# A fused two-FFN and mixer block on one core: another order and other engines for the loading stage

## The chip, the core and the metric

The kernel runs on one core of one Trainium2 chip. Its engines are TensorE (PE in the profile; PEld are its weight loads), VectorE (DVE), ScalarE (ACT), GpSimd (POOL) and SyncE (SP, which here only issues DMAs). Each works through its own list of instructions in order, and semaphores tie the lists together. PSUM, which TensorE writes, has eight banks of 128 x 512 float32. In this kernel GpSimd's operands all lie in SBUF. The metric is the device time in microseconds (us) of one execution, the median of several.

## What is computed

4096 tokens of 128 features go through three residual steps: a mixture-of-experts FFN, a mixer (gate, a 5-tap convolution, a linear recurrence, an output projection, a layer norm) and the same FFN again. All of it is float32. The FFN, with T tokens, 32 experts of 64 hidden units and a shared expert of 128:

```python
logits = tokens @ router_weight.T
scores = sigmoid(logits);  sfc = scores + router_bias
# the best 2 of 4 groups by the sum of their 2 best scores, then the best 4 experts of these
topk_w = scores[chosen] / (sum of them + 1e-20) * 2.5
hidden = silu(tokens @ gate_w[e].T) * (tokens @ up_w[e].T)        # every expert e
mixed  = sum over the chosen e of topk_w * (hidden @ down_w[e].T)
shared = (silu(tokens @ shared_gate_w.T) * (tokens @ shared_up_w.T)) @ shared_down_w.T
x = x + 0.5 * (mixed + shared)                                    # tokens = layernorm(x)
```

The kernel computes every expert for every token and multiplies by a routing weight that is zero for those not chosen.

## The kernel before

**Tiling.** The tokens are 8 blocks of 512. FFN 1 and FFN 4 (the second) of each block make 16 units (`ORDER`), the first four being FFN 1 of blocks 0 to 3. A unit has 17 tiles (`NT`): tile 0 is the shared expert, tiles 1 to 16 are pairs of experts. For a tile TensorE makes a gate and an up product (`up_tiles`, three matmuls of 512 columns each) and three tiles later a down product (`down`). Between them ScalarE takes the silu in place in the gate's bank (`silu_tile`), VectorE multiplies by the routing weights (`weigh_tile`) and by the up product (`hidden_tile`, into one of four `hid` buffers), and the result is split for the next product.

**The split.** Every operand of a matmul is kept as two numbers of type float32r: a high part (a rounding copy, `xT_hi`, `hid_hi`, `wt_hi`, by ScalarE) and a low part, the difference (`xT_lo`, `wt_lo` by VectorE, `hid_lo` by GpSimd). A product is high x high + high x low + low x high.

**The loading stage.** The weights come from HBM as 14 batches of four 128 x 128 tiles (`raw`); `BATCHES` orders them: number 0 is the mixer's and router's weights, 1 the shared expert's, 2 to 13 the experts'. Each is transposed by TensorE into a PSUM bank (`weights(n)`, L1130), copied to `wt_hi` (`weight_high`, L662) and subtracted to `wt_lo` (`weight_low`, L823, VectorE). Of batches 3 to 5 (`BY_SCALAR`) TensorE itself makes the difference: `weights_rest` (L1120) transposes them again and subtracts the high part by a product with the negated identity, and ScalarE copies it. The low parts 6 to 9 are `LOWS_BEHIND`. Batches 10 to 13 are handled within tiles 1, 3, 5 and 7 of unit 0.

Ahead of them TensorE does 14 transposes of the identity (`WARM`, L1316), whose result nobody reads. Beside the weights, block 0's tokens are normalised by VectorE (L1084), transposed by TensorE (L1325), split, and routed: `first_router` (L1209), 12 products of 32 columns, then `route_step` 0 to 25 on VectorE (L893 to L964, ending in `w_tok`). `transpose_route` (L1224) turns `w_tok`, ScalarE copies it (`wT`, L711), and from there it is spread to all partitions in two ways: the first two pairs (`EARLY`) by products with a spreading matrix (L1348) and two ScalarE copies (L809), the rest by a store to HBM and broadcasting loads (L499, L511) in pieces (`CHUNKS`). `constants` (L1042, VectorE) prepares the mixer's taps, bias and decay, which block 0's mixer needs some 98 us in.

**Order.** All of it is written out by hand; no scheduler moves anything. TensorE's list in the loading stage is: 14 transposes, batch 0, batch 1, the token transposes, batch 2, the router, batches 3 to 9 with `weights_rest` and tile 0's products among them, `transpose_route`, batch 9, the spreading, then the units. Within units tables such as `BEGIN` say beside which tile the norms, routers and the mixer go. Some of the lines:

```python
            weights(0)
            weights(1)
            for t in range(TT):
...
            weights(2)
            first_router()
            for i in range(3, LATE):
```

## Time and profile before

| | us |
|---|---|
| median of 3 runs (lowest, highest) | 674.52 (674.22, 674.72) |
| span of the profiled execution | 672.1 |
| TensorE busy | 658.3 (98%) |
| VectorE busy | 550.3 (82%) |
| GpSimd busy | 447.0 (67%) |
| ScalarE busy | 420.2 (63%) |

The span runs from the first to the last instruction of one profiled execution; the median is of other executions and holds what lies around the span too. A busy share is a mean over stages: 98% on TensorE says that it seldom idles, not that each of its instructions was needed or ran at the full clock. Matmuls overlap, so the distance from one start to the next says more than a duration. Of a wait, the profile names the engine and instruction that came last.

### The profile page before, as it was taken

The page shows a single profiled execution, that of the slowest core. Times are in us where ns is not written, and L with a number is a line of the kernel's source. Part 1 is how long each engine was busy: PE and PEld are TensorE (multiplying, and loading weights), DVE is VectorE, ACT ScalarE, POOL GpSimd, SP SyncE. Part 2 cuts the span into 40 slices and gives each one's busy share as a digit, 9 for nine tenths or more (in the row PEclk, how much of TensorE's full clock was granted, in tenths as well). Part 3 has the DMA queues.
Part 4 walks back from the last instruction along what each step waited for, and adds up shares of the span by engine and source line. Part 5 has one row for each costly group of instructions (what it writes and reads, how often), then busy time and mean ns, then how long its engine had stood idle before and what let it go on. Part 6 is the DMA issues. An engine that isn't in the chain of part 4 may idle for free. (4 is left out here: it accounts for less than half of the span.)

```text
span 672.1 us, 10288 instructions
## 1 busy us (share of the span) xinstructions
PE 658.3 (98%) x3061; PEld 532.4 (79%) x3061; DVE 550.3 (82%) x1542; ACT 420.2 (63%) x802; POOL 447.0 (67%) x452
## 2 busy tenths in 40 slices
PE   7999999999999999999999999999999999999997
PEld 6877888888888887888888888888878778777785
DVE  5788889988978887889779798688989967967765
ACT  3666576675576656666567765767576566655554
POOL 2256557875676776866767766868676776676564
PEclk9999999999999999999999999999999999999999
DMA  8672908439092844619075370916509074380461
GB/s 201 147 159 64 223 1 196 92 76 195 5 213 69 182 89 111 144 57 225 22 173 115 89 166 23 228 38 146 125 25 222 9 156 100 82 188 17 112 143 32
DMA packets 60232, 78.30 MB, mean 117 GB/s; under 512 B 8176, under 2 KB 27664, under 8 KB 60176
## 3 DMA queue, kind: packets, MB, share of 16 engines
q1 hardware_dynamic: 59312, 77.49, 51.8%
q8 instruction: 24, 0.39, 0.3%
q10 hardware_dynamic: 864, 0.15, 0.2%
q14 instruction: 32, 0.26, 0.1%
HBM read 74.49 MB, written 3.15 MB: 116 GB/s over the span
## 5 line engine op out<-in xcount | busy, mean ns | idle before, releaser
L572 POOL TENSOR_TENSOR hid_lo<-hid,hid_hi 128x512 fp32r<-128x512 f32 x270 | 348.8, 1296 | 189.5 <-ACT hid_hi L684 189.3
L837 DVE TENSOR_TENSOR weighted<-gate_ps,raw 128x512 f32<-128x512 f32 x256 | 175.1, 684 | 69.4 <-ACT gate_ps L676 62.5
L676 ACT ACTIVATE gate_ps<-gate_ps 128x512 f32<-128x512 f32 x256 | 148.7, 581 | 120.2 <-PE gate_ps L1118 117.0
L684 ACT ACTIVATE hid_hi<-hid 128x512 fp32r<-128x512 f32 x272 | 170.5, 627 | 62.1 <-DVE hid L850 59.7
L850 DVE TENSOR_TENSOR hid<-weighted,up_ps 128x512 f32<-128x512 f32 x256 | 174.3, 681 | 8.0 <-issue 0.5
L1181 PE MATMUL down_ps<-hid_lo,wt_hi 128*128 128x512 f32 x272 | 107.8, 396 | 0.2 <-DVE hid_lo L858 0.2
L1178 PE MATMUL down_ps<-hid_hi,wt_hi 128*128 128x512 f32 x272 | 107.7, 396 | 0.0
L1179 PE MATMUL down_ps<-hid_hi,wt_lo 128*128 128x512 f32 x272 | 107.5, 395 | 0.0
L1116 PE MATMUL gate_ps<-xT_hi,wt_hi 128*128 128x512 f32 x170 | 71.7, 422 | 0.0
L1116 PE MATMUL up_ps<-xT_hi,wt_hi 128*128 128x512 f32 x170 | 68.2, 401 | 2.1 <-DVE hid L850 2.1
L1117 PE MATMUL gate_ps<-xT_lo,wt_hi 128*128 128x512 f32 x170 | 67.2, 395 | 0.0
L1118 PE MATMUL up_ps<-xT_hi,wt_lo 128*128 128x512 f32 x170 | 67.2, 395 | 0.0
L1117 PE MATMUL up_ps<-xT_lo,wt_hi 128*128 128x512 f32 x170 | 67.1, 395 | 0.0
L1118 PE MATMUL gate_ps<-xT_hi,wt_lo 128*128 128x512 f32 x170 | 67.1, 395 | 0.0
L1181 PEld LDWEIGHTS down_ps<-hid_lo,wt_hi 128*128 128x128 f32 x272 | 51.1, 188 | 13.6 <-DVE hid_lo L858 0.9
L1179 PEld LDWEIGHTS down_ps<-hid_hi,wt_lo 128*128 128x128 f32 x272 | 51.1, 188 | 12.2
L1178 PEld LDWEIGHTS down_ps<-hid_hi,wt_hi 128*128 128x128 f32 x272 | 51.1, 188 | 12.1
L1116 PE MATMUL gate_ps<-xT_hi_spare,wt_hi 128*128 128x512 f32 x102 | 42.5, 417 | 0.0
L1116 PEld LDWEIGHTS up_ps<-xT_hi,wt_hi 128*128 128x128 f32 x170 | 31.9, 188 | 13.2 <-DVE hid L850 5.7
L1116 PE MATMUL up_ps<-xT_hi_spare,wt_hi 128*128 128x512 f32 x102 | 40.4, 396 | 0.0
L1117 PE MATMUL gate_ps<-xT_lo_spare,wt_hi 128*128 128x512 f32 x102 | 40.3, 395 | 0.0
L1118 PE MATMUL up_ps<-xT_hi_spare,wt_lo 128*128 128x512 f32 x102 | 40.3, 395 | 0.0
(187 smaller groups left out, 1111.8 us busy)
## 6 DMA issues: line engine op xcount, KB each, us to landing
raw<-wT_hbm SPq DMA_DIRECT2D x96, 512.0 KB, 11.4
raw<-wT_hbm SPq DMA_DIRECT2D x62, 256.0 KB, 4.5
x_ln<-in_L_attn_x SPq DMA_DIRECT2D x8, 256.0 KB, 3.7
x_res<-in_L_attn_x SPq DMA_DIRECT2D x8, 256.0 KB, 3.3
out_x<-x SPq DMA_DIRECT2D x7, 256.0 KB, 2.3
raw<-in_L_ffn_gate_w SPq DMA_DIRECT2D x4, 256.0 KB, 5.7
raw<-in_L_ffn_up_w SPq DMA_DIRECT2D x4, 256.0 KB, 5.0
raw<-in_L_ffn_down_w SPq DMA_DIRECT2D x4, 256.0 KB, 5.1
```

Source lines behind the costliest of these rows:

```text
L572: nc.gpsimd.tensor_tensor(hid_lo[s][:, :], hid[s][:, :], hid_hi[s][:, :].bitcast(F32), ALU.subtract)\
L676: nc.scalar.activation(bank[:, :] if j else silu_sb[:, :], bank[:, :], ACT.Silu).then_inc(silu_done, 1)
L684: nc.scalar.activation(hid_hi[s][:, :], hid[s][:, :], ACT.Copy).then_inc(hid_hi_done, 1)
L837: V.tensor_tensor(weighted[j % 2][:, :], gate_ps[n % BANKS][:, :], wb[:, j - 1, :], ALU.mult)\
L850: V.tensor_tensor(hid[n % RING][:, :], factor[:, :], up_ps[n % BANKS][:, :], ALU.mult)\
L1116: nc.tensor.matmul(dst, w, moving_hi, start=start, stop=False)
L1117: nc.tensor.matmul(dst, w, moving_lo, start=False, stop=False)
L1118: return nc.tensor.matmul(dst, w_lo, moving_hi, start=False, stop=stop)
L1178: nc.tensor.matmul(down_ps[:, :], wt_hi[:, w, :], hid_hi[s][:, :], start=(j == 0), stop=False)
L1179: nc.tensor.matmul(down_ps[:, :], wt_lo[:, w, :], hid_hi[s][:, :], start=False, stop=False)
L1181: nc.tensor.matmul(down_ps[:, :], wt_hi[:, w, :], hid_lo[s][:, :], start=False, stop=(j == NT - 1)).then_inc(down_done, 1)
```

## The change

It rewrites the loading stage and leaves every product of the 16 units as it is.

- *Warm-up.* The transposes of the identity become products of 512 columns with the negated identity (`warm`): eight ahead of batch 0, two behind it, one behind the token transposes. They wait for `neg_ident` too.
- *Block 0's router ahead of the shared weights.* Batch 1 moves from ahead of the token transposes into `first_router`, between the eight products with the high part and the four with the low part; batch 2 goes behind the router. On ScalarE the tanh of the decay and `xT_high` go ahead of batch 1's copy.
- *Seven low parts on GpSimd.* For batches 1 to 7 (`BY_POOL`) ScalarE copies the transposed batch unrounded into a `hid` buffer (`w_staged`), makes the high part from that, and GpSimd subtracts. `weights_rest` and its copies go. VectorE keeps batches 0 and 8 to 13; its first write into each `hid` buffer waits for all seven (`w_lo_pooled`).
- *Constants on GpSimd*, behind the low parts, with a buffer `half`; block 0's mixer waits for them (`mix_const`).
- *Tile 1 early.* The gate and up products of tile 1 follow tile 0's in the loading stage (batch 8 between them), with both silus ahead of `wT_copy`; `transpose_route` goes behind batch 9. The PSUM banks are assigned anew.

The diff, with declarations and the removed bodies left out:

```diff
-WARM = 14
+WARM = (8, 2, 1)
 
 BATCHES = (0, NBATCH - 1) + tuple(range(1, NBATCH - 1))
 
-BY_SCALAR = range(3, 6)
-
-LOWS_BEHIND = (6, 7, 8, 9)
+BY_POOL = range(1, 8)
+
+LOWS_BEHIND = (8, 9)
...
-        setup_banks = 2 * [gate_ps[0], gate_ps[1], mixed] + [gate_ps[1], up_ps[1], mixed, down_ps] + 4 * [mixed]
-        rest_banks = {3: up_ps[0], 4: up_ps[1], 5: down_ps}
+        setup_banks = [gate_ps[0], gate_ps[1], mixed, up_ps[0], down_ps, gate_ps[1], mixed, down_ps, mixed, down_ps]
+        setup_banks += 4 * [mixed]
...
-                        sp.wait_ge(w_rest, max(min(hi + 1, BY_SCALAR[-1] + 1) - BY_SCALAR[0], 1))
...
+            for i in BY_POOL:
+                pool.wait_ge(w_hi_done, i + 1)
+                nc.gpsimd.tensor_tensor(batch(wt_lo, i), hid[i % RING][:, :], batch(wt_hi, i).bitcast(F32), ALU.subtract)\
+                  .then_inc(w_lo_pooled, 1)
+            mixing = Steps(pool, mix_const, 0)
+            mixing.done(nc.gpsimd.memset(half[:, :], 0.5))
+            pool.wait_ge(taps_loaded, 16 * 3)
+            mixing.wait()
+            mixing.done(nc.gpsimd.tensor_tensor(taps_half[:, :], taps[:, :], half[:, :], ALU.mult))
+            mixing.done(nc.gpsimd.tensor_tensor(cbias_half[:, :], cbias[:, :], half[:, 0:1], ALU.mult))
+            pool.wait_ge(a_done, 1)
+            pool.wait_ge(dve_const, 4)
+            mixing.done(nc.gpsimd.tensor_tensor(decay[:, :], ones[:, :], a_tanh[:, 0:1].broadcast_to([P, BLK]),
+                                                ALU.mult))
+            mixing.wait()
+            mixing.done(nc.gpsimd.memset(decay[:, :].rearrange("p (s t) -> p s t", s=SB)[:, :, 0:1], 0.0))
+            assert mixing.n == MIX_CONST
...
             def weight_high(i):
                 act.wait_ge(w_transposed, i + 1)
-                nc.scalar.activation(batch(wt_hi, i), setup_bank(i), ACT.Copy).then_inc(w_hi_done, 1)
-
-            def weight_low(i):
-                act.wait_ge(w_rest, i - BY_SCALAR[0] + 1)
-                nc.scalar.activation(batch(wt_lo, i), rest_bank(i), ACT.Copy).then_inc(w_lo_copied, 1)
+                whole = setup_bank(i)
+                if i in BY_POOL:
+                    if i - RING in BY_POOL:
+                        act.wait_ge(w_lo_pooled, i - RING - BY_POOL[0] + 1)
+                    whole = hid[i % RING][:, :]
+                    nc.scalar.activation(whole, setup_bank(i), ACT.Copy).then_inc(w_staged, 1)
+                    act.wait_ge(w_staged, i - BY_POOL[0] + 1)
+                nc.scalar.activation(batch(wt_hi, i), whole, ACT.Copy).then_inc(w_hi_done, 1)
...
-                    if before is not None or j > 0:
+                    if before is not None or j > 1:
...
             for i in range(LATE):
                 weight_high(i)
-                if i == 8:
-                    wT_copy(1, 0)
-                    silu_tile(1, 0, 0)
-                if i - 1 in BY_SCALAR:
-                    weight_low(i - 1)
-                if i == 1:
+                if i == 0:
+                    act.wait_ge(taps_loaded, 16 * 3)
+                    nc.scalar.activation(a_tanh[:, :], a_raw[:, :], ACT.Tanh).then_inc(a_done, 1)
                     xT_high(1, 0)
                 if i == 1:
-                    act.wait_ge(taps_loaded, 16 * 3)
-                    nc.scalar.activation(a_tanh[:, :], a_raw[:, :], ACT.Tanh).then_inc(a_done, 1)
-                if i == 2:
                     silu_logits(1, 0)
+                if i == 8:
+                    silu_tile(1, 0, 0)
+                    silu_tile(1, 0, 1)
+                    wT_copy(1, 0)
...
                 if n >= RING:
                     dve.wait_ge(hid_lo_done, n - RING + 1)
+                else:
+                    dve.wait_ge(w_lo_pooled, len(BY_POOL))
...
-            def constants():
...
                     if (k, m) == ORDER[0] and j == 0:
-                        for n in LOWS_BEHIND[2:]:
+                        for n in LOWS_BEHIND:
...
             weight_low(0)
             xT_low(1, 0)
-            weight_low(1)
-            weight_low(2)
-            constants()
...
-            for n in LOWS_BEHIND[:2]:
-                weight_low(n)
...
-            def weights_rest(n):
...
-                if n in (3, 4, 5):
-                    pe.wait_ge(w_lo_done, lows_by_vector(n - 2))
-                elif n == 6:
-                    pe.wait_ge(w_hi_done, 5)
-                elif n == 7:
-                    pe.wait_ge(w_lo_copied, 2)
-                elif n == 8:
-                    pe.wait_ge(w_hi_done, 6)
-                elif n == 9:
-                    pe.wait_ge(w_lo_copied, 3)
+                if n in (5, 6, 7):
+                    pe.wait_ge(w_staged, {5: 1, 6: 2, 7: 4}[n])
+                elif n in (8, 9):
+                    pe.wait_ge(w_staged, n - 2)
                 elif n >= LATE:
                     pe.wait_ge(w_lo_done, lows_by_vector(n))
                 for t in range(4):
-                    last = nc.tensor.transpose(setup_bank(n)[:, t * P:(t + 1) * P],
-                                               raw[:, min(4 * b + t, down_tile(0)), :], ident[:, :])
+                    last = nc.tensor.matmul(setup_bank(n)[:, t * P:(t + 1) * P],
+                                            raw[:, min(4 * b + t, down_tile(0)), :], ident[:, :], is_transpose=True,
+                                            start=True, stop=True)
                 last.then_inc(w_transposed, 1)
...
+            def warm(n):
+
+                for _ in range(n):
+                    nc.tensor.matmul(routed[:, :], neg_ident[:, :],
+                                     neg_ident[:, :].unsqueeze(1).broadcast_to([P, TT, P]), start=True, stop=True)
...
+                weights(1)
                 pe.wait_ge(xT_lo_done[1], 1)
...
             pe.wait_ge(pool_const, 4)
-            for n in range(WARM):
-                nc.tensor.transpose(routed[:, 0:P], ident[:, :], ident[:, :])
+            pe.wait_ge(dve_const, 6)
+            warm(WARM[0])
             weights(0)
-            weights(1)
+            warm(WARM[1])
             for t in range(TT):
                 if t < TT - 1:
                     pe.wait_ge(first_normed, t + 1)
...
                     pe.wait_ge(ln_normed[1], 1)
                 last = nc.tensor.transpose(side[:, t * P:(t + 1) * P], normed[1][:, t, :], ident[:, :])
             last.then_inc(xn_transposed[1], 1)
-            weights(2)
+            warm(WARM[2])
             first_router()
-            for i in range(3, LATE):
-                if i == LATE - 1:
-                    transpose_route(1, 0)
+            for i in range(2, LATE):
+                if i == 8:
+                    pe.wait_ge(w_lo_done, 1)
+                    pe.wait_ge(w_staged, 3)
+                    pe.wait_ge(w_hi_done, 4)
+                    pe.wait_ge(w_lo_pooled, 1)
+                    up_tiles(1, 0, 0)
+                if i == 9:
+                    pe.wait_ge(route[1], LOGITS_READ)
+                    pe.wait_ge(w_staged, 5)
+                    pe.wait_ge(w_lo_pooled, 4)
+                    up_tiles(1, 0, 1)
                 weights(i)
-                if i == 3:
-                    pe.wait_ge(dve_const, 6)
-                if i == 5:
-                    pe.wait_ge(route[1], LOGITS_READ)
-                if i - 1 in BY_SCALAR:
-                    weights_rest(i - 1)
-                if i == 8:
-                    pe.wait_ge(w_hi_done, 4)
-                    pe.wait_ge(w_lo_copied, 1)
-                    pe.wait_ge(w_lo_done, lows_by_vector(2))
-                    up_tiles(1, 0, 0)
+            transpose_route(1, 0)
...
-            pe.wait_ge(w_lo_copied, len(BY_SCALAR))
-            pe.wait_ge(w_lo_done, 3 + LOWS_BEHIND.index(7) + 1)
```

How the lists change, at three places. TensorE, from its first instruction to the first products of block 0's router. Before (`routed<-ident` is the warm-up, `raw` a weight batch, `normed` the tokens, L1216 and L1217 the router):

```order
L1317 MATMUL routed<-ident 128x128 x14
L1146 MATMUL gate_ps<-ident,raw 128x128 x8
L1325 MATMUL side<-ident,normed 128x128 x4
L1146 MATMUL mixed<-ident,raw 128x128 x4
L1216 MATMUL up_ps<-wt_hi,xT_hi 128x32
L1217 MATMUL up_ps<-wt_lo,xT_hi 128x32
```

After (L1204 is the warm-up, L1137 a weight batch, L1324 the tokens):

```order
L1204 MATMUL routed<-neg_ident 128x512 x8
L1137 MATMUL gate_ps<-ident,raw 128x128 x4
L1204 MATMUL routed<-neg_ident 128x512 x2
L1324 MATMUL side<-ident,normed 128x128 x4
L1204 MATMUL routed<-neg_ident 128x512
L1214 MATMUL up_ps<-wt_hi,xT_hi 128x32
```

The token transposes now stand behind one weight batch and ten products without input from HBM; batches 1 and 2, which stood around them, come behind the router's first eight products and behind the router.

GpSimd, from its first work on block 0's norm to its first low part of unit 0 (`hid_lo`). Before:

```order
L643 TENSOR_TENSOR rstd<-var_eps,neg_half 128x4
L644 AFFINE_SELECT beat_at<-zeros 128x16
L650 AFFINE_SELECT spread<-zeros 128x128 x8
L572 TENSOR_TENSOR hid_lo<-hid,hid_hi 128x512
L579 TENSOR_TENSOR neg_mean<-zeros,meanvar 128x4
L581 TENSOR_TENSOR var_eps<-meanvar,eps 128x4
```

After (L656 are the weights' low parts, L659 to L669 the constants):

```order
L642 TENSOR_TENSOR rstd<-var_eps,neg_half 128x4
L643 AFFINE_SELECT beat_at<-zeros 128x16
L649 AFFINE_SELECT spread<-zeros 128x128 x8
L656 TENSOR_TENSOR wt_lo<-hid,wt_hi 128x512 x7
L659 MEMSET half 128x5
L662 TENSOR_TENSOR taps_half<-taps,half 128x5
L663 TENSOR_TENSOR cbias_half<-cbias,half 128x1
L666 TENSOR_TENSOR decay<-ones,a_tanh 128x512
L669 MEMSET decay 128x2
L571 TENSOR_TENSOR hid_lo<-hid,hid_hi 128x512
```

Seven subtractions and five small operations now stand ahead of `hid_lo`.

ScalarE, the end of the loading stage, to the first `hid_hi` (L664 and L687 are weight batches, `silu_sb` and `gate_ps` the silus, `wT` the routing weights, `raw<-side` and `raw<-routed` the early copies, the first of them batch 8). Before:

```order
L664 ACTIVATE wt_hi<-mixed 128x512
L711 ACTIVATE wT<-side 128x128
L676 ACTIVATE silu_sb<-gate_ps 128x512
L664 ACTIVATE wt_hi<-down_ps 128x512
L809 ACTIVATE raw<-side 128x512
L809 ACTIVATE raw<-routed 128x512
L676 ACTIVATE gate_ps<-gate_ps 128x512
L684 ACTIVATE hid_hi<-hid 128x512
```

After (L685 is batch 7's unrounded copy):

```order
L685 ACTIVATE hid<-down_ps 128x512
L687 ACTIVATE wt_hi<-hid 128x512
L687 ACTIVATE wt_hi<-mixed 128x512
L695 ACTIVATE silu_sb<-gate_ps 128x512
L695 ACTIVATE gate_ps<-gate_ps 128x512
L730 ACTIVATE wT<-side 128x128
L687 ACTIVATE wt_hi<-down_ps 128x512
L828 ACTIVATE raw<-side 128x512
L828 ACTIVATE raw<-routed 128x512
L703 ACTIVATE hid_hi<-hid 128x512
```

Both silus now stand ahead of `wT`, and the first `hid_hi` follows the early copies with no silu between.

## Rows read from the trace of the kernel before

**Rows 1.** Page: span, busy time, granted clock in 40 slices (9 is full).

```profile
span 672.1 us, 10288 instructions
...
PE 658.3 (98%) x3061; PEld 532.4 (79%) x3061; DVE 550.3 (82%) x1542; ACT 420.2 (63%) x802; POOL 447.0 (67%) x452
...
PEclk9999999999999999999999999999999999999999
```

**Rows 2.** Waits of TensorE, whole span: total us, times, longest.

```profile
PE side L1226 <- DVE w_tok L964: 2.6, 4, 0.9
...
PE mixed L1146 <- DVE wt_lo L825: 0.2, 1, 0.2
```

**Rows 3.** Chain that ended last: start us, us, what (a typical piece).

```profile
631.78 0.23 PE up_ps L1116
```

**Rows 4.** TensorE in order of time: start us, us, what, idle before it.

```profile
1.64 3.25 PE L1317 MATMUL routed<-ident 128*128 128x128 f32 x14 [1.64 <-POOL ident L638]
5.58 1.11 PE L1146 MATMUL gate_ps<-ident,raw 128*128 128x128 f32 x4 [0.70 <-DMA raw<-in_L_ffn_router_weight]
9.15 1.12 PE L1146 MATMUL gate_ps<-ident,raw 128*128 128x128 f32 x4 [2.46 <-DMA raw<-in_L_ffn_shared_down_w]
10.06 1.06 PE L1325 MATMUL side<-ident,normed 128*128 128x128 f32 x4
...
13.53 1.01 PE L1220 MATMUL up_ps<-wt_hi,xT_lo 128*128 128x32 f32 x4
...
16.96 0.78 PE L1127 MATMUL up_ps<-wt_hi,neg_ident 128*128 128x512 f32 x1
...
20.57 0.48 PE L1127 MATMUL down_ps<-wt_hi,neg_ident 128*128 128x512 f32 x1
...
24.47 1.13 PE L1348 MATMUL side<-wT,spread 128*128 128x128 f32 x8
...
27.73 0.60 PE L1146 MATMUL mixed<-ident,raw 128*128 128x128 f32 x4
28.09 0.48 PE L1116 MATMUL gate_ps<-xT_hi,wt_hi 128*128 128x512 f32 x1
```

**Rows 5.** VectorE in order of time.

```profile
6.40 1.25 DVE L1084 TENSOR_SCALAR normed<-x_ln,meanvar,rstd 128x128 f32<-128x128 f32 x4 [1.22 <-POOL rstd L643]
...
14.66 0.29 DVE L893 TENSOR_SCALAR tiny<-up_ps 128x128 f32<-128x128 f32 x1
...
23.25 0.38 DVE L964 SCALAR_TENSOR_TENSOR w_tok<-chosen,routed 128x128 f32<-128x128 f32 x1
...
24.92 0.69 DVE L850 TENSOR_TENSOR hid<-silu_sb,up_ps 128x512 f32<-128x512 f32 x1 [0.18 <-ACT silu_sb L676]
...
37.75 0.69 DVE L837 TENSOR_TENSOR weighted<-gate_ps,raw 128x512 f32<-128x512 f32 x1 [0.19 <-DMA raw<-wT_hbm]
...
40.63 0.69 DVE L837 TENSOR_TENSOR weighted<-gate_ps,raw 128x512 f32<-128x512 f32 x1 [1.41 <-ACT gate_ps L676]
```

**Rows 6.** ScalarE in order of time.

```profile
24.05 0.28 ACT L711 ACTIVATE wT<-side 128x128 f32<-128x128 f32 x1 [1.39 <-PE side L1226]
...
27.72 0.62 ACT L684 ACTIVATE hid_hi<-hid 128x512 fp32r<-128x512 f32 x1
...
97.55 0.60 ACT L768 ACTIVATE val_pad<-side 128x512 f32<-128x512 f32 x1 [0.45 <-PE side L1118]
98.18 0.78 ACT L774 ACTIVATE mixed<-val_pad,cbias_half,taps_half 128x512 f32<-128x512 f32 x1
```

**Rows 7.** GpSimd in order of time.

```profile
28.49 1.30 POOL L572 TENSOR_TENSOR hid_lo<-hid,hid_hi 128x512 fp32r<-128x512 f32 x1 [19.95 <-ACT hid_hi L684]
```

**Rows 8.** Two lines of code: ns min/median/max, first and last start.

```profile
L927 DVE TENSOR_TENSOR routed<-gsum x16: 225/614/1128, 19.6 to 620.4; 128x64 f32<-128x64 f32 x16
...
L572 POOL TENSOR_TENSOR hid_lo<-hid,hid_hi x270: 1267/1297/1325, 28.5 to 662.8; 128x512 fp32r<-128x512 f32 x135
```

**Rows 9.** DMA issues of 9.5 to 10.2 us: xcount, KB, us to landing.

```profile
raw<-in_L_ffn_down_w SPq DMA_DIRECT2D x1, 256.0 KB, 5.0
```

More of the change, by code:

```diff
@@ L65, in lows_by_vector @@
 def lows_by_vector(n):
-    return sum(i not in BY_SCALAR for i in range(n))
+    return sum(i not in BY_POOL for i in range(n))
 def pair_tile(q):
@@ L170, in macaron_kernel @@
         decay = sb("decay", [P, BLK])
+        half = sb("half", [P, K])
         silu_sb = sb("silu_sb", [P, BLK])
@@ L256, in macaron_kernel @@
         a_done = sem("a_done")
+        mix_const = sem("mix_const")
         w_transposed = sem("w_transposed")
@@ L259, in macaron_kernel @@
         w_lo_done = sem("w_lo_done")
-        w_rest = sem("w_rest")
-        w_lo_copied = sem("w_lo_copied")
+        w_staged = sem("w_staged")
+        w_lo_pooled = sem("w_lo_pooled")
         wT_stored = sem("wT_stored")
@@ L442, in macaron_kernel @@
         MIX = K + 1
+        MIX_CONST = 5
         block = ctx.enter_context(nc.Block())
-        setup_banks = 2 * [gate_ps[0], gate_ps[1], mixed] + [gate_ps[1], up_ps[1], mixed, down_ps] + 4 * [mixed]
-        rest_banks = {3: up_ps[0], 4: up_ps[1], 5: down_ps}
+        setup_banks = [gate_ps[0], gate_ps[1], mixed, up_ps[0], down_ps, gate_ps[1], mixed, down_ps, mixed, down_ps]
+        setup_banks += 4 * [mixed]
         early_bank = [side, routed]
@@ L455, in setup_bank @@
             return setup_banks[n][:, :]
-        def rest_bank(n):
-            return rest_banks[n][:, :]
         def batch(t, i):
@@ L773, in unit @@
                             act.wait_ge(mix, b * MIX)
+                        else:
+                            act.wait_ge(mix_const, MIX_CONST)
                         nc.scalar.activation(conv, val_pad[:, :, 0:SEQ], ACT.Identity,
@@ L848, in hidden_tile @@
                     dve.wait_ge(hid_lo_done, n - RING + 1)
+                else:
+                    dve.wait_ge(w_lo_pooled, len(BY_POOL))
                 factor = weighted[j % 2] if j else silu_sb
@@ L972, in conv_tap @@
                     dve.wait_ge(first_tap_done, i + 1)
+                    if i == 0:
+                        dve.wait_ge(mix_const, MIX_CONST)
                 else:
@@ L1040, in beside @@
                         norm_meanvar(k, b)
-            def constants():
-                dve.wait_ge(taps_loaded, 16 * 3)
-                const.done(V.tensor_scalar(taps_half[:, :], taps[:, :], 0.5, None, ALU.mult))
-                const.done(V.tensor_scalar(cbias_half[:, :], cbias[:, :], 0.5, None, ALU.mult))
-                dve.wait_ge(a_done, 1)
-                const.wait()
-                const.done(V.tensor_scalar(decay[:, :], ones[:, :], a_tanh[:, 0:1], None, ALU.mult))
-                const.wait()
-                const.done(V.memset(decay[:, :].rearrange("p (s t) -> p s t", s=SB)[:, :, 0:1], 0.0))
-                const.wait()
             def unit(k, m):
@@ L1118, in product @@
                 return nc.tensor.matmul(dst, w_lo, moving_hi, start=False, stop=stop)
-            def weights_rest(n):
-                pe.wait_ge(w_hi_done, n + 1)
-                for t in range(4):
-                    tile = min(4 * BATCHES[n] + t, down_tile(0))
-                    nc.tensor.matmul(rest_bank(n)[:, t * P:(t + 1) * P], raw[:, tile, :], ident[:, :],
-                                     is_transpose=True, start=t == 0, stop=False)
-                nc.tensor.matmul(rest_bank(n), neg_ident[:, :],
-                                 batch(wt_hi, n), start=False, stop=True).then_inc(w_rest, 1)
             def weights(n):
@@ L1248, in unit @@
                         pe.wait_ge(w_lo_done, lows_by_vector(NBATCH))
-                    if before is not None or j > 0:
+                    if before is not None or j > 1:
                         up_tiles(k, m, j)
```

## Prediction

> **What bounds the kernel now.** I read the page's head first: TensorE is busy 658.3 of 672.1 us [rows 1]. Next its waits: 2.6 us in four places for routing weights, 0.2 us for one weight batch's low part [rows 2]. The chain of waits that ended last is, over most of its length, products of 512 columns 0.23 us apart [rows 3]. So what is saved before TensorE's stream closes up is saved at the end, unless another engine takes it back. Then TensorE in order of time [rows 4]. Two things stand out. It sits 2.46 us before 9.15 because the shared weights' batch is written ahead of the transposes of block 0's normalised tokens, which so start at 10.06, though VectorE has normalised the last tile by 7.65 (6.40 + 1.25 [rows 5]). And the same product L1127 takes 0.78 us at 16.96 and 0.48 at 20.57. The granted clock prints full in every slice [rows 1], so I go by durations: everything up to 16.96 ran at the 1.2 GHz level, everything from 20.57 at 2.4. Before the rise TensorE had done transposes and 32-column products, then the first 512-column one at 16.96. On VectorE the route of block 0 runs from 14.66 to 23.63 without a pause and ends the loading stage [rows 5]; GpSimd stands idle 19.95 us until 28.49 [rows 7].
>
> The profiled span is 672.1 us, the median of the runs 674.5; 2.4 us lie outside the span and I leave them as they are. All sums are in the span's time.
>
> **The change part by part.**
>
> *Warm-up.* It starts at 2.4 (the negated identity needs 0.2 us more than the identity) instead of 1.64. A chain of 512-column products at the low level is not in the trace; bounds are 0.23 us each (their spacing at the high level [rows 3]) and 0.78 (one alone at the low level [rows 4]). I take 0.46, twice the spacing, as the level is half. Eight: 3.7 us, to 6.1. Batch 0's transposes take 0.9 (9.15 to 10.06) to 7.0, two more products to 7.9. They start 0.5 later than at 5.58, which is hidden: the next transposes wait for the normalised tokens until 7.65 in any case.
>
> *Block 0's router first.* The token transposes start at 7.9 instead of 10.06; a group of four ends after 1.06 us at the low and 0.60 at the high level [rows 4], so at 8.5 to 9.0. A copy of 0.60 [rows 6] makes it 9.2 or 9.7. Then 12 router products 0.22 apart (the last four take 1.01 at 13.53) and the shared batch's transposes among them, 0.9, with a tail of 0.2 (9.15 + 1.12 against 10.06): 3.7 us at the low level, and half, 1.9 with the tail, at the high one. The logits are read at 11.2 (high) or 13.4 (low), not 14.66. VectorE comes free for it: two low parts and the four constants that stood ahead are gone. I take the high level: the warm-up is 3.7 us of what preceded the rise at 20.57, only denser. Gain 3.5 us here.
>
> *The route.* It lasts 8.97 us (14.66 to 23.63). Now GpSimd works beside it. L927 takes 225 ns alone and up to 1128 ns beside GpSimd's products [rows 8], median 614: cost 0 to 0.9, taken 0.4. The routing weights are there at 11.2 + 9.0 + 0.4 = 20.6.
> The Trainium skill, "SBUF — State Buffer", section "SBUF: two separate sides", says that VectorE instructions with two SBUF inputs and GpSimd ones that read SBUF hold a shared port in turn, for a whole instruction. The spread of L927 agrees. By that rule alone the price could be one full GpSimd low part, about 1.3, and the result 671.7.
>
> *Low parts on GpSimd.* Twelve transposes and three products go from TensorE, which there waits for others anyway; seven batches are copied twice by ScalarE and subtracted by GpSimd. An operation that waits for the copy before it starts 0.63 us after it (97.55, 98.18 [rows 6]); a copy takes 0.60: 1.23 us a batch, and 1.13 with the next one's start overlapped. GpSimd's subtraction of the same shape takes 1.27 to 1.33 in all 270 cases [rows 8], so GpSimd sets the pace. Batch 1 is transposed at 10.7 (9.2 + 8 x 0.11 + 0.4 + 0.2), its high part done at 11.95; the silu of the logits, priced as the 128-column copy of 0.28 [rows 6], stands ahead of batch 2, whose high part is done at 13.5. Six low parts of 1.30 later the seventh ends at 21.3. The new wait is VectorE's: its first hidden tile waits for all seven, and behind it are the low parts 8 and 9 and everything of unit 0. So 21.35 against 24.92 [rows 5]: 3.6 earlier. GpSimd's constants follow: if the one of 512 columns takes the 1.3 of [rows 8] and the four small ones as much as 0.3 each, they end by 23.8; GpSimd is next wanted at 24.7, so I cost them at nothing, and with that cover gone at up to 2.5.
>
> *The tail of the stage on TensorE.* Batch 7 waits for the fourth copy, at 12.25 + 2 x 1.13 + 0.6 = 15.1; its data is issued by 10.2 and lands by 15.2 [rows 9]. With 0.4 a batch and 6 x 0.23 = 1.4 a tile: batch 7 15.5, tile 0 16.9, batch 8 (waits for its bank, the sixth copy, 17.4) 17.8, tile 1 19.2, batch 9 19.6. Then it waits for the routing weights: 20.6, transposed 21.0, copied by ScalarE at 21.05 to 21.35 (which by 12.25 + 6 x 1.13 + 3 x 0.6 = 20.9 has done its pairs of copies, batch 8 and two silus). Before, that copy ended at 24.33 [rows 6]. The spreading products, two sets of 1.13 less the tail, take 1.85, to 23.25. The second early copy (0.2 of tail and 0.6) ends at 24.1, and the first hidden high part now follows at once, against 27.72 [rows 6], and GpSimd's first hidden low part at 24.75 against 28.49 [rows 7]: 3.7 earlier. TensorE starts tile 2 at 23.25 + 0.36 (27.73 to 28.09) = 23.6 against 28.09: 4.5 earlier.
>
> *The sum.* 4.5 on TensorE, 3.6 to 3.7 on the others; the smaller one counts, since soon after, TensorE waits for the low part of batch 12 (the 0.2 of [rows 2]), behind GpSimd's first low part. What is next late is the second piece of the spread routing weights by DMA: it was used at 37.75 as it landed [rows 5], 13.4 after 24.33. Now 21.35 + 13.4 = 34.75, against 37.75 - 3.7 = 34.05: 0.7 late on VectorE, whose next weighting, at 40.63, had 1.41 idle before it [rows 5]; that takes it up. I cost it at nothing, at most 0.7. After that all waits are relative. 674.5 - 3.7 = **670.8 us**. Its own bounds: L927 at nothing 670.3, at 0.9 671.3, the DMA 0.7 more: 670.0 to 672.0.
>
> **The rivals.**
>
> *The level falls again in the lull.* Between 11.2 and 15.1 TensorE has only groups of four transposes, spaced by the loads. For it: at the low level transposes and 32-column products up to 16.96 didn't raise it. Against: after 20.57 no row shows a fall, though TensorE idles up to 0.9 at a time [rows 2]. Price: tile 0 runs 16.0 to 18.8, batch 8 to 19.65; if the level is back within the 3.6 us that it took from 16.96 to 20.57, tile 1 ends at 21.05 and the copy of the routing weights at 22.2, 0.85 later: 671.6. If it is back only at tile 1's end (22.4), the copy ends at 23.5: 673.0. Taken: 672.2.
> The Trainium skill, "TensorE: Matmul & The Clock Gate", Part 4, says that the full level does not engage for transposes as for products; by it this rival and the warm-up's success would both come true. The trace agrees for the rise only; no run here shows a fall.
>
> *The warm-up does not raise the level* (the change doesn't do what it says). Logits at 13.4, routing weights at 22.8, batches 2 to 6 at 0.9 each, tile 0 at 18.3 at the low level, tile 1 to 23.2, copy of the routing weights at 24.3 as before; only the place of the hidden high part behind the early copies gains, 0.7: 673.8. It is also what products of 0.78 each would give.
>
> *Slower.* The level falls and is still low when the spreading products are issued. Place: from 24.1 on; there the point of decision lies, as until then other engines cover it. Price: those 1.85 become 3.7, batch 10 0.9, so tile 2 starts at 28.7, 0.6 late, and each tile at the low level adds 1.4: with one tile 676.5. Against: one 512-column product at 16.96 and another before 20.57 went with a rise, and tiles 0 and 1 are twelve.
>
> *Given back downstream.* VectorE, for whose routing weights TensorE waits 0.9 in the worst case [rows 2], may be the bound of units 0 and 1 and take up most: 673.5.
>
> **How the numbers follow.** Forecast 0.46, fall with return 0.26, no rise 0.15, slower 0.08, given back 0.05. 0.2% (1.35 us) is about what a measurement can tell from no change, so the first two count as faster (with 0.02 of the third), the third and fifth as same. Faster 0.74, same 0.18, slower 0.08. Range: from 669.5 (below 670.0 for durations that differ between executions) to 674.0, which takes in the third and leaves out the slower and the edges.
>
> **What would show it.** Right: eight products at 2.4, spaced 0.43 or so at first and 0.23 by the end; token transposes near 8; first step of the route near 11.2; last of seven GpSimd low parts near 21.3; GpSimd's first hidden low part near 24.7; tile 2 of unit 0 near 23.6. Wrong: products of tile 0 spaced 0.43; a route of over 9.9 us; VectorE's first hidden tile waiting for GpSimd beyond 22; TensorE waiting in units 0 and 1 by over 1 us more than the 2.6 and 0.2.

## The result, and the profile after

The change brought 664.08 us (663.96 to 664.37) against 674.37 (673.62 to 674.72) for the kernel before on the same chip: a ratio of 0.985 (0.983 to 0.986), 10.3 us less. The forecast was 3.7 us less and its range began at 669.5: the direction is right, the size is not. The page's head, to be held against [rows 1]:

```profile
span 661.9 us, 10261 instructions
...
PE 644.7 (97%) x3043; PEld 524.0 (79%) x3043; DVE 547.4 (83%) x1534; ACT 422.2 (64%) x806; POOL 456.7 (69%) x464
...
PEclk9999999999999999999999999999999999999999
```

TensorE is busy 13.6 us less, though its matmuls are only 18 fewer (3061 to 3043 records). First the stage that was rewritten. TensorE in order of time (start us, us, what, idle before it), against [rows 4]:

```profile
2.54 3.75 PE L1204 MATMUL routed<-neg_ident 128*128 128x512 f32 x8 [2.54 <-DVE neg_ident L1088]
...
7.80 0.75 PE L1324 MATMUL side<-ident,normed 128*128 128x128 f32 x4
8.31 0.48 PE L1204 MATMUL routed<-neg_ident 128*128 128x512 f32 x1
9.24 0.28 PE L1214 MATMUL up_ps<-wt_hi,xT_hi 128*128 128x32 f32 x1 [0.45 <-ACT xT_hi L718]
9.37 0.26 PE L1215 MATMUL up_ps<-wt_lo,xT_hi 128*128 128x32 f32 x1
9.48 0.26 PE L1214 MATMUL up_ps<-wt_hi,xT_hi 128*128 128x32 f32 x1
...
15.92 0.39 PE L1124 MATMUL gate_ps<-xT_lo,wt_hi 128*128 128x512 f32 x1
16.15 0.39 PE L1125 MATMUL gate_ps<-xT_hi,wt_lo 128*128 128x512 f32 x1
...
22.01 1.13 PE L1346 MATMUL side<-wT,spread 128*128 128x128 f32 x8 [0.46 <-ACT wT L730]
...
24.22 0.48 PE L1123 MATMUL gate_ps<-xT_hi,wt_hi 128*128 128x512 f32 x1
```

The eight products are 0.44 us apart ((6.09 - 2.54) / 8, the next start being 6.09); by 9.24 the router's products are 0.11 apart, not 0.22; tile 0's at 15.92 are 0.23 apart, so the level did not fall in the lull. Tile 2 of unit 0 starts at 24.22, not 28.09. VectorE, against [rows 5], then GpSimd, against [rows 7]:

```profile
11.20 0.29 DVE L914 TENSOR_SCALAR tiny<-up_ps 128x128 f32<-128x128 f32 x1 [1.29 <-PE up_ps L1219]
...
16.15 1.22 DVE L948 TENSOR_TENSOR routed<-gsum 128x64 f32<-128x64 f32 x1
...
20.79 0.38 DVE L985 SCALAR_TENSOR_TENSOR w_tok<-chosen,routed 128x128 f32<-128x128 f32 x1
21.14 0.69 DVE L871 TENSOR_TENSOR hid<-silu_sb,up_ps 128x512 f32<-128x512 f32 x1
...
35.68 0.69 DVE L856 TENSOR_TENSOR weighted<-gate_ps,raw 128x512 f32<-128x512 f32 x1 [1.28 <-DMA raw<-wT_hbm]
```

```profile
12.19 8.82 POOL L656 TENSOR_TENSOR wt_lo<-hid,wt_hi 128x512 fp32r<-128x512 f32 x7 [3.71 <-ACT wt_hi L687]
...
25.33 1.29 POOL L571 TENSOR_TENSOR hid_lo<-hid,hid_hi 128x512 fp32r<-128x512 f32 x1 [2.64 <-ACT hid_hi L703]
```

GpSimd's first hidden low part comes 3.16 us earlier (28.49 before), and the routing weights of block 1 are transposed 3.17 earlier (56.42 against 59.59). So in these two executions 3.2 us come from the loading stage. The other 7 come after it, where the program is the same. There the distance between products differs. Six products from one to the next, before and then after (in each fence the first and the last start):

```profile
205.03 0.40 PE L1178 MATMUL down_ps<-hid_hi,wt_hi 128*128 128x512 f32 x1
...
206.43 0.40 PE L1116 MATMUL up_ps<-xT_hi,wt_hi 128*128 128x512 f32 x1
```

```profile
206.45 0.39 PE L1123 MATMUL up_ps<-xT_hi,wt_hi 128*128 128x512 f32 x1
...
207.81 0.39 PE L1123 MATMUL gate_ps<-xT_hi,wt_hi 128*128 128x512 f32 x1
```

1.40 us before, 1.36 after. Over all distances under 0.25 us from a product of 512 columns to the next start, between 30 and 640 us (some 2,250 in each trace), the mean is 233.1 ns before and 228.3 after. The granted clock prints full in both.

### The profile page after: what moved, and what is told of

Read it like the earlier page. It is cut to its first block and busy times, and to the rows that moved or that the text cites. A ratio compares the mean times of both kernels' runs of the same rounds, so it can differ in the third digit from the quotient of the medians.

```text
span 661.9 us, 10261 instructions
## 1 busy us (share of the span) xinstructions
PE 644.7 (97%) x3043; PEld 524.0 (79%) x3043; DVE 547.4 (83%) x1534; ACT 422.2 (64%) x806; POOL 456.7 (69%) x464
## 5 line engine op out<-in xcount | busy, mean ns | idle before, releaser
L1170 PE MATMUL down_ps<-hid_hi,wt_hi 128*128 128x512 f32 x272 | 106.3, 391 | 0.0
L1171 PE MATMUL down_ps<-hid_hi,wt_lo 128*128 128x512 f32 x272 | 105.9, 389 | 0.0
L1125 PE MATMUL gate_ps<-xT_hi_spare,wt_lo 128*128 128x512 f32 x102 | 39.9, 391 | 0.0
```

The lines of the kernel that those rows point to most:

```text
L1125: return nc.tensor.matmul(dst, w_lo, moving_hi, start=False, stop=stop)
L1170: nc.tensor.matmul(down_ps[:, :], wt_hi[:, w, :], hid_hi[s][:, :], start=(j == 0), stop=False)
L1171: nc.tensor.matmul(down_ps[:, :], wt_lo[:, w, :], hid_hi[s][:, :], start=False, stop=False)
```

## Experiments: why the products are faster

A product has two operands in SBUF, the memory of all tiles here but the PSUM banks: a stationary one of 128 columns, which TensorE loads as weights, and a moving one, here of 512 columns. Theory A: the new buffer `half`, 20 bytes a partition, takes 32 bytes in SBUF and moves all tiles declared after it. The program's own addresses: the weights' tiles `wt_hi` and `wt_lo` start on a multiple of 128 in both kernels; the moving operands (`hid_hi`, `hid_lo`, `xT_hi`, `xT_lo`) lay 32 bytes short of a multiple of 256 away from them before, and lie on one after. Theory B: the faster products come from the new warm-up, the new instruction stream or the chip.

**e1_pad32**, the kernel before with one line more:

```diff
         decay = sb("decay", [P, BLK])
+        pad = sb("pad", [P, K])
```

> The kernel before, with one unused buffer of 20 bytes per partition (it takes 32) declared between decay and silu_sb; no instruction differs. It moves silu_sb and every tile declared after it, all moving operands of the 512-column products among them, from 32 bytes past a multiple of 64 to a multiple of 64. Theory A (place of the tiles): products of 512 columns follow each other 0.228 us apart instead of 0.233, some 2,600 of them, so the time falls by about 7 us, to 667.5 (666 to 669). Theory B (the faster products after the change come from its new instruction stream, its warm-up, or the chip): spacing 0.233, time 674.4, ratio 1.000 within 0.002.

Measured: 667.25 us, ratio 0.989 (0.988 to 0.991); mean distance 228.1 ns. Six products take 1.36 here:

```profile
208.68 0.39 PE L1180 MATMUL down_ps<-hid_hi,wt_lo 128*128 128x512 f32 x1
...
210.04 0.39 PE L1118 MATMUL gate_ps<-xT_lo,wt_hi 128*128 128x512 f32 x1
```

**e2_half_last**, the changed kernel with `half` declared behind the last tile:

```diff
-        half = sb("half", [P, K])
...
         wT = {k: sb(f"wT{k}", [P, P]) for k in (1, 4)}
+        half = sb("half", [P, K])
```

> The changed kernel with its buffer half declared behind the last tile, so that every tile lies where it lay before the change; no instruction differs but for addresses. Theory A: spacing of the products back to 0.233 us, time 664.1 + 7 = 671 (670 to 672), which is what is left of the change: the loading stage's 3.2 to 3.7 us. Theory B: spacing 0.228, time 664.1.

Measured: 671.33 us, ratio 0.9965 (0.9951 to 0.9980); mean distance 233.1 ns, six products 1.40:

```profile
208.42 0.40 PE L1125 MATMUL up_ps<-xT_hi,wt_lo 128*128 128x512 f32 x1
...
209.82 0.40 PE L1125 MATMUL gate_ps<-xT_hi,wt_lo 128*128 128x512 f32 x1
```

**e3_pad64**, the kernel before with `pad = sb("pad", [P, 16])` in the same place:

> The kernel before with an unused buffer of 64 bytes per partition in the same place: the tiles move, but stay 32 bytes past a multiple of 64. Theory A in the form that only the remainder by 64 counts: spacing 0.233 us, 674.4, ratio 1.000 within 0.002. If any move of the tiles changes the price of a product (say through what they share with other engines), or if the remainder by 128 counts, it is 0.228 and about 667.5, or something between. Theory B: 674.4.

Measured: 674.55 us, ratio 0.9998 (0.9988 to 1.0007), 233.2 ns.

The three settle it between A and B: the shift alone, without any instruction changed, brings 7.4 us (674.62 to 667.25); the change without the shift brings 2.4 by the ratio and 3.3 by the medians. Not every shift does it: e3 leaves the moving tiles 32 bytes past a multiple of 256 away from the weights. I took the moving operand's own start, by 64 bytes, for what decides, and that was my next mistake.

**e4_probe** and **g1_probe** add products behind the last transposes of the changed kernel, with the operands' starts varied by columns of `wt_hi` (one operand at a time in e4, both together too in g1, whose lines these are):

```diff
+            for g, (w, x) in enumerate(((0, 0), (0, 8), (8, 0), (8, 8), ...)):
+                for _ in range(60):
+                    nc.tensor.matmul(banks[g % 2][:, :], flat[:, w:w + P], flat[:, 512 + x:1024 + x],
+                                     start=True, stop=True)
```

> The changed kernel with products added behind its last transposes on TensorE, their results read by nobody: groups of 20 products of 512 columns whose moving operand starts 0, 8, 16, 24, 4, 12, 0 and 8 float32 columns past a multiple of 64 bytes; two groups with the moving operand at 0 and the stationary one at 8 and at 0; then twice four transposes and 12 products at 0. No other engine works there. Theory A: 0.227 us a product at 0 and 16, 0.233 at 8, 24, 4 and 12; the stationary operand's place costs nothing or less. Theory B: all groups equal. Of the stretches after transposes at 0.233 in the changed kernel: if they come from the transposes, the first few of the 12 products show 0.233, if from other engines' work, all show 0.227. The span grows by about 45 us.

Measured: from start to start the groups of 20 took 4.64, 4.67, 4.59, 4.67, 4.63, 4.66, 4.58 and 4.67 us, and those with the stationary operand 8 columns off or at 0 took 4.66 and 4.56. So the stationary operand's place counts as well, against what A expected. After four transposes six products were slower in one group and all but the last one or two of twelve in the other, with no other engine working.

> The changed kernel with products added behind its last transposes on TensorE, read by nobody, no other engine working: groups of 60 products of 512 columns, the stationary operand w and the moving one x float32 columns past a multiple of 64 bytes, (w, x) = (0,0), (0,8), (8,0), (8,8), (0,16), (0,4), (0,12), (0,32), (0,480), (480,480), (0,0); 32 and 480 bring the start to multiples of 256 and 2048 bytes. If only the remainder by 64 counts: 0.227 us each in the groups (0,0), (0,16), (0,32), (0,480) and (480,480), 0.233 in the others, (8,8) too if the two prices overlap, 0.240 if they add. If larger multiples count, the last groups are cheaper still. Then, twice: four products of 128 columns, not transposes, and 20 of 512 at (0,0), a wait of TensorE for its own last product, and 20 more. The first products after the transposes in e4_probe went 0.233 apart until some eight had passed. If transposes cause that, all here are at 0.227; if any pause or short product does, the first some after both show 0.233.

Groups (0,8), (8,0), (8,8) and the start of (0,16):

```profile
671.87 14.17 PE L1367 MATMUL up_ps<-wt_hi 128*128 128x512 f32 x60
685.87 14.16 PE L1367 MATMUL gate_ps<-wt_hi 128*128 128x512 f32 x60
699.86 13.79 PE L1367 MATMUL up_ps<-wt_hi 128*128 128x512 f32 x60
713.50 13.89 PE L1367 MATMUL gate_ps<-wt_hi 128*128 128x512 f32 x60
```

14.00, 13.99 and 13.64 us: with either operand shifted a product costs 0.233, with both 0.227. It isn't the moving operand's own place that counts but how far the two lie apart. (0,32) took 13.94, so 128 bytes apart isn't good either. After four products of 128 columns that are not transposes two or three products were slower too, and after a pause six and eleven, so it is no property of transposes.

**g2_probe**, the same with one operand shifted in finer steps, 40 products each:

> The changed kernel with products added behind its last transposes, read by nobody, no other engine working: groups of 40 products of 512 columns, the stationary operand on a multiple of 128 bytes, the moving one 2048 bytes further plus 0, 1, 2, 4, 8, 16, 24, 32, 48, 64, 80, 96, 112, 120, 124, 128 and 256 float32 columns. In g1_probe the groups (0,0), (8,8) and (480,480), where both operands start at the same place within 2048 bytes, settled at 0.2267 us a product, and those 128 bytes apart at 0.232, so the first theory (the moving operand's own remainder by 64) fell. Theory G (what counts is how far the two starts are apart, within 512 bytes): 0.227 at 0, 128 and 256 columns, 0.229 to 0.2335 at all others. Theory H (within 256 bytes): 0.227 at 64 columns too. Theory I (within 2048 bytes): 128 and 256 columns cost 0.229 or more; but the changed kernel has differences of all multiples of 512, and its products settle at 0.227, which speaks against it.

Columns 8, 16, 24, 32, 48, 64 and the start of 80:

```profile
695.14 9.49 PE L1365 MATMUL gate_ps<-wt_hi 128*128 128x512 f32 x40
704.48 9.31 PE L1365 MATMUL up_ps<-wt_hi 128*128 128x512 f32 x40
713.63 9.49 PE L1365 MATMUL gate_ps<-wt_hi 128*128 128x512 f32 x40
722.96 9.49 PE L1365 MATMUL up_ps<-wt_hi 128*128 128x512 f32 x40
732.29 9.48 PE L1365 MATMUL gate_ps<-wt_hi 128*128 128x512 f32 x40
741.61 9.27 PE L1365 MATMUL up_ps<-wt_hi 128*128 128x512 f32 x40
750.72 9.34 PE L1365 MATMUL gate_ps<-wt_hi 128*128 128x512 f32 x40
```

Mean of one product, the first ten of each group left out:

| bytes apart | ns |
|---|---|
| 0, 256, 512, 1024 | 226.7 |
| 496 | 226.7 |
| 64, 320 | 228.9 |
| 16 | 231.7 |
| 384 | 232.3 |
| 8, 32, 96, 128, 192, 448, 480 | 233.3 to 233.4 |
| 4 | 236.7 |

Theory H, the distance within 256 bytes, holds here but for 496 (and 384 lies 1 ns from 128). The whole kernel says the same:

**h1_shift256**, the changed kernel with 256 unused bytes behind `half`:

> The changed kernel with 256 unused bytes per partition behind half: all moving operands still lie on a multiple of 64 and of 256, but start 256 bytes away from the weights' tiles within 512. First theory (the moving operand's remainder by 64 decides) and theory H (the distance within 256 bytes): spacing 0.228 us, 664.1, ratio to before as the changed kernel's, 0.985. Theory G (the distance within 512 bytes): spacing 0.229 to 0.2335, 665 to 671.

Measured: 663.59 us, ratio 0.984 (0.982 to 0.985), 228.2 ns: as the changed kernel, so theory G fell. **h2_minus16** tried to use the point at 496, where the products settled at once:

```diff
-        wt_hi = sb("wt_hi", [P, NBATCH * 4, P], F32R)
-        wt_lo = sb("wt_lo", [P, NBATCH * 4, P], F32R)
+        wt_hi, wt_lo = (sb(name, [P, NBATCH * 4 * P + 64], F32R)[:, 4:4 + NBATCH * 4 * P]
+                        .rearrange("p (n d) -> p n d", d=P) for name in ("wt_hi", "wt_lo"))
```

> The changed kernel with the weights' tiles wt_hi and wt_lo 16 bytes further on in their buffers (these 256 bytes longer), so that every moving operand of the 512-column products starts 16 bytes before a multiple of 256 away from its weights instead of on one. In g2_probe the distance of 496 bytes was the one other than multiples of 256 at which products settled at 0.2267 us, and there they did so from the second one on, where 0, 256 and 512 needed about ten. If the distance counts within 256 bytes and the early settling is a property of it: the ten or so slower products behind each group of transposes go, spacing 0.227 instead of 0.228, time 661 to 663.5. If the early settling was chance: spacing 0.228, 664, ratio to before 0.983 to 0.986. If 496 doesn't stand for 240: 0.2333, 670 to 672.

Measured: 669.73 us, ratio 0.993 (0.991 to 0.994), 232.1 ns. Here `wt_hi` lies 496 and `wt_lo` 240 bytes from the moving tiles within 512, and products with `wt_hi` were as slow (232.2) as those with `wt_lo`. So the point at 496 doesn't carry over, and why it was fast there stays open. **f4_pad_y** moved `y_hi`, `y_lo` and the routing weights' tiles by 32 bytes:

> The changed kernel with 32 unused bytes per partition behind val_pad, whose 2080 bytes leave y_hi, y_lo, the routing weights' tiles and all behind them 32 bytes past a multiple of 64; with it they lie on a multiple. y_hi and y_lo are stationary operands of 96 products of 128 columns in the mixer; a group of 20 products with the stationary operand 32 bytes off took 4.66 us against 4.56 in e4_probe, 0.005 us each. If that holds for these too: 0.5 us off, 663.6; if short products hide it: 664.1, ratio to the changed kernel 1.000 within 0.001.

Measured: 664.27 us, ratio 0.984 (0.983 to 0.986): no difference. By what g1 and g2 show it was no test: `y_hi` went from 32 to 64 bytes past a multiple of 256 away from the weights, and neither is one. None of the three beats the changed kernel by more than their intervals.

## Experiments: the loading stage

**f1_old_warm**, the changed kernel with the old warm-up:

```diff
-            pe.wait_ge(dve_const, 6)
-            warm(WARM[0])
+            for n in range(14):
+                nc.tensor.transpose(routed[:, 0:P], ident[:, :], ident[:, :])
             weights(0)
-            warm(WARM[1])
...
-            warm(WARM[2])
+            pe.wait_ge(dve_const, 6)
             first_router()
```

> The changed kernel with the warm-up of before: 14 transposes of the identity ahead of batch 0, and none of the three later products. Theory C (the 512-column products raise TensorE's level before the router): without them the router's products are 0.22 us apart instead of 0.11, tile 0's products run at 0.43 or so, and the time rises by 2 to 3 us, to 666 to 667. Theory D (order and engines alone make the loading stage's gain, the level matters little as TensorE waits for others there): 664.1, within 1.0.

Measured: 665.91 us, ratio 0.9863, by the ratios 1.2 us more than the changed kernel's 0.9846. The router's products were 0.21 apart, the route began at 12.34 instead of 11.20, tile 2 at 25.33 instead of 24.22. But tile 0 ran at 0.23, since the level rose without the products. The batches behind the router:

```profile
12.14 1.11 PE L1137 MATMUL mixed<-ident,raw 128*128 128x128 f32 x4
13.05 1.06 PE L1137 MATMUL up_ps<-ident,raw 128*128 128x128 f32 x4
13.90 0.78 PE L1137 MATMUL down_ps<-ident,raw 128*128 128x128 f32 x4
14.52 0.60 PE L1137 MATMUL gate_ps<-ident,raw 128*128 128x128 f32 x4
```

0.91 and 0.85 from one to the next, then 0.62 and 0.44 (the next starts at 14.96). Between theories C and D: C's mechanism, near D's price.

The Trainium skill, "TensorE: Matmul & The Clock Gate", Part 4, says that the full level does not engage for transposes. Here it did: up to 13.9 TensorE had done nothing but transposes and 32-column products. In e1, which has the old list, 14 transposes alone had done it: batch 0's transposes behind them took 0.66 us in all, and those after the next wait 1.11 again.

```profile
5.59 0.66 PE L1147 MATMUL gate_ps<-ident,raw 128*128 128x128 f32 x4 [0.71 <-DMA raw<-in_L_ffn_router_weight]
9.64 1.11 PE L1147 MATMUL gate_ps<-ident,raw 128*128 128x128 f32 x4 [3.40 <-DMA raw<-in_L_ffn_shared_down_w]
```

In the kernel before, with the same list, the first of the two took 1.11 as well (5.58, [rows 4]). So when the level rises differs between executions of one list, and f1's trace is one of them.

**f2_batch1_ahead**, `weights(1)` moved from `first_router` to behind `weights(0)`:

> The changed kernel with batch 1, the shared expert's weights, back ahead of block 0's token transposes; the warm-up stays. Those transposes then wait for the batch's transfer, until some 9.2 + 0.9 us as before the change, instead of starting at 7.8. Theory C (the order is worth what the prediction said of it, some 2 us on the route): first step of the route near 13.3 instead of 11.2, time up by about 2 us, to 666. Theory D (GpSimd's low parts set the end of the stage, not the route): 664.1 to 664.8.

Measured: 668.33 us, ratio 0.990, by the ratios 3.5 us more than the changed kernel's: C's mechanism and more than its price. The route began at 14.95, not at 13.3. Part of that is the level: behind the eight products batch 0's transposes were 0.11 apart, batch 1's, after a wait of 3.2 us, 0.21 (from 9.89), and so were block 0's token transposes; by the router, at 13.40, it was 0.11 again. So f2 changes the order and, with the wait, the level too. Later the level fell once more. TensorE by windows (us, busy, granted clock, DMA share, GB/s), and two rows in order of time:

```profile
24.00:26.00 2.00, 0.73 (x4) 1.00 0.00 0
26.00:28.00 2.00, 2.00 (x14) 0.63 0.16 41
28.00:30.00 2.00, 2.00 (x10) 0.52 0.46 129
```

```profile
28.33 1.06 PE L1137 MATMUL mixed<-ident,raw 128*128 128x128 f32 x4
29.05 0.78 PE L1123 MATMUL gate_ps<-xT_hi,wt_hi 128*128 128x512 f32 x1
29.62 0.53 PE L1124 MATMUL gate_ps<-xT_lo,wt_hi 128*128 128x512 f32 x1
```

Behind a stretch in which TensorE did one transposition, at 24.81, and then the first spreading products, the granted clock is 0.63 and 0.52, mostly the 1.2 GHz level: the second set of spreading products takes 1.71 us (26.62 to 28.33; 0.90 in the changed kernel, 22.97 to 23.87), and the first products of tile 2 are 0.57 and 0.37 apart. That is the rival "slower", at its place, in a neighbour of the change; on TensorE it costs 0.8 in the spreading, 0.4 in batch 10 (0.72 against 0.35) and 0.4 in the products, 1.6 in all.

It comes in the changed kernel's own list too. f4 and e4 have the same list in this stage, and in both traces the level fell in the spreading. In f4 the second set takes 1.56 us, and the first products of tile 2 are 0.57, 0.43 and 0.37 apart:

```profile
22.35 1.77 PE L1347 MATMUL routed<-wT,spread 128*128 128x128 f32 x8
23.91 1.06 PE L1138 MATMUL mixed<-ident,raw 128*128 128x128 f32 x4
24.63 0.78 PE L1124 MATMUL gate_ps<-xT_hi,wt_hi 128*128 128x512 f32 x1
25.20 0.63 PE L1125 MATMUL gate_ps<-xT_lo,wt_hi 128*128 128x512 f32 x1
```

That is 1.6 us on TensorE, of which 0.7 reached GpSimd's first hidden low part (25.42, from a spreading begun at 21.39 instead of 22.01). f4's time shows no loss.

**f3_lows_behind_route**, one wait more on GpSimd:

```diff
+            pool.wait_ge(route[1], ROUTE)
             for i in BY_POOL:
```

> The changed kernel with GpSimd's seven low parts made to wait for the end of block 0's route, so that VectorE has the route's 26 steps without GpSimd's products beside it. Theory E (sharing with GpSimd lengthens the route by 1.0 us, from the 8.97 of before to the 9.97 of after): route 9.0 us, its end near 20.2 instead of 21.2. Theory F (the route's length comes from other things): route 9.9 or 10.0. The time itself rises in both, by some 8 us, as the low parts end after 29 instead of 21: near 672.

Measured: 670.24 us, ratio 0.994, 6 us up rather than 8. The route takes 8.98 us (10.69 to 19.67):

```profile
15.65 0.23 DVE L949 TENSOR_TENSOR routed<-gsum 128x64 f32<-128x64 f32 x1
...
19.29 0.38 DVE L986 SCALAR_TENSOR_TENSOR w_tok<-chosen,routed 128x128 f32<-128x128 f32 x1
```

Theory E holds, and one instruction carries the price: 0.23 us here against the 1.22 at 16.15 beside GpSimd, 0.99 of the 0.99 between the routes (9.97, 8.98). By the rule of the Trainium skill, "SBUF — State Buffer", section "SBUF: two separate sides", that I had weighed, the price was up to one whole GpSimd instruction of 1.3; the trace agrees.

## The prediction, step by step

- **The warm-up.** Right in its end, wrong in its course: I had expected 0.23 spacing by the eighth product; all eight ran at 0.44, and the rise came by 8.31. Token transposes 7.80 (7.9 predicted), route 11.20 (11.2).
- **The route.** 0.4 taken for L927's sharing, up to 0.9 bounded; it was 0.99, and the 9.9 named as a sign of error was passed by 0.07.
- **GpSimd's low parts.** The seventh ends at 21.01 (21.3), the constants at 22.7 (23.8). VectorE's first hidden tile does not wait for them beyond 21.14.
- **The end of the stage.** Tile 2 24.22 (23.6), hidden low part 25.33 (24.75), 3.16 earlier instead of 3.7: the route's 0.6 passed on. But one execution does not tell 3.2 from 3.7: in three profiled executions of the old list (the kernel before, e1, e3) this low part came at 28.49, 28.98 and 29.25, in eight of the new one (the changed kernel, e2, e4, f4, g1, g2, h1, h2) between 24.72 and 25.61. The broadcast piece came 1.28 late on VectorE instead of 0.7 and was taken up: the shift is still 3.17 at 56.42.
- **The step that failed** is the one sentence "After that all waits are relative". It takes the price of every later product as unchanged, because the change leaves those instructions as they are. Their addresses it did not leave. The change declares `half` ahead of all these tiles, and I read it as a buffer of 20 bytes. This term was set at nothing and measured 7.4 us (e1). With the tiles back in place the forecast of 670.8 stands against 671.33 (e2; 672.2 by the ratio).
- **The rivals.** No fall in the lull, and in the changed kernel's trace no spell at the low level in the spreading; f4 and e4 show that the same list can have one. So the mechanism of "slower" is there, at its place, but was priced too high: its terms come to 3.8 us on TensorE, f4 shows 1.6, and 0.7 passed on. "Does not raise the level" was priced at 3.0 us above the forecast (673.8) and is worth 1.2 (f1): I had kept tile 0 at the low level. Nothing was given back downstream: e2, with the old price of a product, was 3.77 ahead of the kernel before at the first hidden low part (24.72) and 3.6 at the end of its span (668.5).
- **Of the shift itself,** some 2,250 counted distances times 4.8 ns make 10.8 us, of which 7.4 reach the end (e1). TensorE's waits from 30 us on rose from 5.3 to 6.6 in e1. Set side by side product by product, which e1 and the kernel before allow as their lists are the same, the distances that are under 0.25 in both are 11.6 us shorter in e1, and the rest 5.0 longer, 2.2 of it in 21 distances that were under 0.25 before, which leaves the 6.6 between the two spans (672.1 and 665.5). So the faster TensorE is held up at more places; by which engine at each was not followed.

## What to carry to other kernels

Where one engine does thousands of equal instructions, compare the addresses of its operands before and after any change that declares a buffer, and run the buffer alone first: 32 bytes were worth twice what the rewriting was, or more (7.4 us against 2.4 to 3.3). Declare the tiles that TensorE reads together so that stationary and moving operands start a multiple of 256 bytes apart. And a gain that appeared evenly over a stretch that the change didn't touch was a change of price here, not of waits: measure the distance between equal instructions there first.

## What the runs showed of the hardware

- A product of 512 float32r columns costs 226.7 ns when its two operands start a multiple of 256 bytes apart in a partition, and 228.9 to 236.7 at the other distances tried but one, 496 (g2). Both operands' places count, not the absolute address: 13.64 us for 60 with both shifted, 14.00 with one (g1). What conflicts inside was not shown. After transposes, short products or a pause two to eleven products pass before 226.7 is reached (e4, g1). In the changed kernel those from the thirteenth on behind such a place have a mean of 227.0, the earlier ones of 229.8, and that makes its mean 228.3.
- A page can print the granted clock as full where it was not: between 14 and 16 us the same instruction list printed 0.50 in e1 and 1.00 in the kernel before, with the router's products before it 0.21 to 0.22 us apart in both. Durations tell the level, the printed clock tells its changes.
- Two executions of one list can have different levels at the same instruction: batch 0's transposes took 1.11 us in the kernel before and 0.66 in e1, the second set of spreading products 0.90 in the changed kernel and 1.56 in f4. So a claim on the level from one trace holds for that execution.
